# A sort of edges by matrix products: its table of next places kept as three bf16 parts and brought up to date by the vector engine

## The reference

```python
edge_index = jnp.stack([src, dst])
# in the first layer: row, col = edge_index
out = jax.ops.segment_sum(msg, row, num_segments=N)      # grouped by src
```

## Time and profile before

| | us |
|---|---|
| median of 3 runs | 12618.34 (12607.03 to 12618.74) |
| the profiled execution | 12618.56 |
| its span in the profile | 12616.8 |
| mean granted clock of PE, share of full speed | 0.591 |
| busy: POOL / DVE / PE / ACT | 6532.0 / 5345.2 / 3962.2 / 2582.5 |

### The profile page before, as it was taken

One profiled execution on the slowest core, in us unless ns is written; L12 is line 12 of the kernel. 1 busy time (PEld: TensorE's weight loads), 2 busy tenths in 40 slices (PEclk: granted clock), 3 DMA queues, 4 the chain that ended last, 5 costly groups with the idle time before them and its releaser, 6 DMA issues. The chain is left out here.

```text
span 12616.8 us, 82629 instructions
## 1 busy us (share of the span) xinstructions
PE 3962.2 (31%) x19153; PEld 2596.1 (21%) x19153; DVE 5345.2 (42%) x6339; ACT 2582.5 (20%) x3818; POOL 6532.0 (52%) x6784
## 2 busy tenths in 40 slices
PE   2667501896333333344000100010002000015877
PEld 2555401453111111244000100010001000003544
DVE  6222285334555555277455322222223466652111
ACT  0333253232222322111000011100110233320000
POOL 0666576002777777374777477747773655540000
PEclk9555555897555555577555555555555555557899
DMA  6000022666888888200666311121111222225899
GB/s 276 3 3 3 12 91 78 230 269 229 270 265 267 266 265 270 55 0 0 176 188 187 67 38 37 36 20 38 37 37 18 60 80 80 81 70 200 323 384 359
DMA packets 586456, 1693.37 MB, mean 134 GB/s; under 512 B 267163, under 2 KB 321858, under 8 KB 568289
## 3 DMA queue, kind: packets, MB, share of 16 engines
q0 software_dynamic: 292720, 608.23, 18.7%
q1 hardware_dynamic: 229648, 722.30, 15.7%
q10 hardware_dynamic: 63952, 361.30, 7.3%
HBM read 1016.07 MB, written 675.24 MB: 134 GB/s over the span
## 5 line engine op out<-in xcount | busy, mean ns | idle before, releaser
L1991 POOL DMA_INDIRECT ring<-tab_gat,at x2352 | 2235.8, 951 | 1082.5 <-issue 719.7
L706 POOL DMA_INDIRECT ring<-z_stn,at x1568 | 1508.2, 962 | 1406.2 <-POOLq L703 912.0
L2159 PE MATMUL keys<-spot,ones 128*128 128x128 f32 x6 | 2.3, 487 | 3766.2 <-PEq L2158 3766.2
L1503 PE MATMUL pair_acc<-pair_w,pair_cell 32*112 32x384 f32 (+1 forms) x1120 | 780.3, 878 | 1261.3 <-PEq L1500 1261.3
L560 POOL DMA_INDIRECT sorted<-rows,at x784 | 759.3, 968 | 761.8 <-POOLq L558 528.5
L706 POOL DMA_INDIRECT ring<-z_conv,at x784 | 767.4, 979 | 386.7 <-issue 249.9
L1082 POOL DMA_INDIRECT adj<-val_a,at_a x784 | 766.0, 977 | 335.3 <-issue 255.2
L1249 PE MATMUL acc<-tile,parts 128*96 128x448 f16 (+1 forms) x3430 | 729.4, 361 | 257.5 <-DVE parts L1173 139.8
L2159 PEld LDWEIGHTS keys<-spot,ones 128*128 128x128 f32 x6 | 1.5, 311 | 3766.9 <-issue 3766.9
L2085 DVE COPY peak<-peak 128x6 f32<-128x6 f32 x112 | 19.8, 176 | 1672.4 <-DVEq L2084 1672.4
L878 PE MATMUL acc<-tail,hot 128*128 128x49 f32 (+4 forms) x588 | 145.8, 432 | 1797.9 <-PEq L876 1797.9
(11 more groups left out here) (453 smaller groups left out, 10619.7 us busy)
## 6 DMA issues: line engine op xcount, KB each, us to landing
tile<-adj SPq DMA_DIRECT2D x490, 784.0 KB, 21.4
z_stn<-block ACTq DMA_DIRECT2D x245, 800.0 KB, 3.3
z_conv<-pair_block ACTq DMA_DIRECT2D x224, 700.0 KB, 6.2
run_gat<-out_rows SPq DMA_DIRECT2D x56, 1596.0 KB, 5.5
adj<-zero SPq DMA_DIRECT2D x49, 1568.0 KB, 38.6
run_basis<-out_rows SPq DMA_DIRECT2D x28, 1750.0 KB, 5.8
ring<-tab_gat,at POOLq DMA_INDIRECT x2352, 2.4
run_gat<-out_rows SPq DMA_DIRECT2D x56, 672.0 KB, 3.1
```

Of the source, the lines that this page charges most:

```text
L706: g.indirect_dma_start(out=view(bufs[b], k), out_offset=None, in_=table, in_offset=bass.IndirectOffsetOnAxis(ap=at[n][b][:, k:k + 1], axis ...
L1503: last = pe.matmul(self.acc[g][0:self.nodes, n, 0:(hi - lo) * self.fo], self.cell[:, :], cols, start=True, stop=True)
L1991: g.indirect_dma_start(out=ring[b][:, k, :], out_offset=None, in_=tab_gat, in_offset=bass.IndirectOffsetOnAxis(ap=at[b][:, k:k + 1], axis= ...
```

## The change

The table of next places, `first`, stays in SBUF in f32, and beside it stands a copy as three bf16 tiles, `parts`: the rounded value, the rounded rest, and the rest of that. DVE makes them (`split`), and DVE adds the lap's sums to the table too: PE's product with the identity and ACT's copy of the table are gone. The f32 look-up product becomes three bf16 products, one for each part, and ACT copies each transposed unit only once, as bf16. PE waits at the head of a lap for `parts_ready` instead of `table_ready`.

```diff
-                lo_rows = sb(st, "lo_rows", [P, ST, P])
-                lo_rows_b = sb(st, "lo_rows_b", [P, ST, P], BF16)
+                lo_rows = sb(st, "lo_rows", [P, ST, P], BF16)
+                parts = [sb(st, f"parts{b}", [P, 3, ST, NT], BF16) for b in range(2)]
+                rest = sb(st, "rest", [P, ST, NT])
@@ DVE @@
+                    def split(b):
+                        v.tensor_copy(parts[b][:, 0, :, :], first[b][:, :, :]).then_inc(dve_step, 1)
+                        v.wait_ge(dve_step, 1)
+                        v.sem_inc(dve_step, -1)
+                        v.tensor_tensor(rest[:, :, :], first[b][:, :, :], parts[b][:, 0, :, :], ALU.subtract).then_inc(dve_step, 1)
...
+                        v.tensor_copy(parts[b][:, 1, :, :], rest[:, :, :]).then_inc(dve_step, 1)
...
+                        v.tensor_tensor(parts[b][:, 2, :, :], rest[:, :, :], parts[b][:, 1, :, :], ALU.subtract).then_inc(dve_step, 1)
...
+                        v.sem_inc(sem("parts_ready"), 1)
@@
-                    v.sem_inc(sem("first_made"), 1)
-                    v.sem_inc(sem("table_ready"), 1)
+                    split(0)
                     v.sem_inc(sem("found_free"), 1)
                     make(0, 0)
                     with v.Fori(0, steps) as it:
                         for b in range(2):
                             make(1 - b, it * 2 + b + 1)
+                            v.wait_ge(sem("table_summed"), 1)
+                            v.sem_inc(sem("table_summed"), -1)
+                            v.tensor_tensor(halves(first[1 - b]), wide(table), halves(first[b]), ALU.add).then_inc(dve_step, 1)
+                            v.wait_ge(dve_step, 1)
+                            v.sem_inc(dve_step, -1)
+                            split(1 - b)
                             v.wait_ge(sem("found_ready"), 1)
@@ ACT @@
-                            a.wait_ge(sem("table_summed"), 1)
-                            a.sem_inc(sem("table_summed"), -1)
-                            a.copy(halves(first[1 - b]), wide(table)).then_inc(act_step, 1)
...
-                            a.sem_inc(sem("table_ready"), 1)
                             def take(lo, hi):
...
-                                a.copy(lo_rows_b[:, lo:hi, :], turned[:, 0:hi - lo, :])
                                 a.copy(lo_rows[:, lo:hi, :], turned[:, 0:hi - lo, :]).then_inc(act_step, 1)
@@ PE @@
-                    def carried(b):
-                        for h in range(2):
-                            pe.matmul(table[:, h, 0:half * NT], ident[:, :],
-                                      first[b][:, h * half:(h + 1) * half, :].rearrange("p j k -> p (j k)"), start=True, stop=False)
...
                             take("hot_made")
-                            take("table_ready")
-                            carried(b)
-                            summed(b, True).then_inc(sem("table_summed"), 1)
+                            take("parts_ready")
+                            for j in range(ST):
+                                last = pe.matmul(cell(table, j), hot_lo[b][:, j, :], hot_hi[b][:, j, :], start=True, stop=True)
+                            last.then_inc(sem("table_summed"), 1)
...
                             for j in range(ST):
-                                pe.matmul(cell(found, j), lo_rows[:, j, :], first[b][:, j, :], start=True, stop=False)
+                                for k in range(3):
+                                    pe.matmul(cell(found, j), lo_rows[:, j, :], parts[b][:, k, j, :], start=(k == 0), stop=False)
                                 last = pe.matmul(cell(found, j), earlier[:, j, :], hot_hi[b][:, j, :], start=False, stop=True)
```

More of the change, by code:

```diff
@@ L452, in _ @@
                         for b in range(2):
-                            a.wait_ge(sem("table_summed"), 1)
-                            a.sem_inc(sem("table_summed"), -1)
-                            a.copy(halves(first[1 - b]), wide(table)).then_inc(act_step, 1)
-                            a.wait_ge(act_step, 1)
-                            a.sem_inc(act_step, -1)
-                            a.sem_inc(sem("table_ready"), 1)
                             def take(lo, hi):
@@ L483, in _ @@
                 def _(pe):
[L485 to L488, removed]
                     for h in range(2):
@@ L497, in _ @@
                             pe.sem_inc(sem("hot_made"), -1)
-                            summed(b, False).then_inc(sem(f"hot_free{b}"), 1)
+                            for j in range(ST):
+                                last = pe.matmul(cell(table, j), hot_lo[b][:, j, :], hot_hi[b][:, j, :], start=False, stop=False)
+                            last.then_inc(sem(f"hot_free{b}"), 1)
                     for h in range(2):
@@ L506, in _ @@
                     pe.matmul(cell(found, 1), ones[:, :], deg[:, :], start=True, stop=True).then_inc(sem("digits_summed"), 1)
-                    pe.wait_ge(sem("first_made"), 1)
-                    pe.sem_inc(sem("first_made"), -1)
-                    def carried(b):
-                        for h in range(2):
-                            pe.matmul(table[:, h, 0:half * NT], ident[:, :],
-                                      first[b][:, h * half:(h + 1) * half, :].rearrange("p j k -> p (j k)"), start=True, stop=False)
                     def turn(b, lo, hi):
@@ L523, in match @@
                         for j in range(lo, hi):
-                            last = pe.matmul(gram[:, j - lo, :], lo_rows_b[:, j, :], lo_rows_b[:, j, :], start=False, stop=(j == hi - 1))
+                            last = pe.matmul(gram[:, j - lo, :], lo_rows[:, j, :], lo_rows[:, j, :], start=False, stop=(j == hi - 1))
                         last.then_inc(sem("gram_ready"), 1)
```

## The result

| | before | after |
|---|---|---|
| median, us | 12618.54 (12607.03 to 12621.81) | 12415.55 (12393.57 to 12423.62) |
| profiled execution, us | 12618.56 | 12409.41 |
| its span | 12616.8 | 12407.7 |
| first and last scatter of the sort, us | 297.06 and 1523.38 | 290.83 and 1332.97 |
| one lap of 14 scatters | 22.00 | 18.65 |

The ratio is 0.9838, with an interval of 0.9821 to 0.9855: 203 us less. The forecast was 12408.0, within 12386 to 12512.

A forecast was written before the change was run, and what follows sets the result against it. PE and ACT together were taken to set the 22.0 us lap, with POOL next at 17.8. 12618.6 less 218.6 (train of scatters) and 5.3 (start), plus 13.3 (slower scatters), gives 12408.0 us; range 12386 to 12512.

The forecast's parts named there:

- The bound: Sort loop: PE and ACT set the 22.0 us lap; afterwards POOL's 14 scatters, 17.8 us, would; 80 in 100.
- PE and ACT: Their lap in the sort falls to 13.1 us mean: 0.65 + 9.95 + 2.5, the last for 56 bf16 products.
- rival 1: Look-ups: PE stays the bound, products in one cell 0.169 us apart; lap 20.1, about 12512 us; 9 in 100.
- rival 3: Look-ups: each product waits for its predecessor in the cell, 0.244 us; lap 24.3, 12747 us; 4 in 100.
- DVE: Table update adds 4.85 us a lap, at most 5.6; DVE's lap 11.1 us, beside PE, so not the bound.
- The start: Before the loop: splitting the first table costs 3.7 us, yet the first scatter comes at 291.7, 5.3 us earlier.
- The cost on POOL: Scatters beside DVE's new SBUF work: 17 ns longer each, 784 of them, 13.3 us.
- The bound of 76 us: Upper bound of the scatters' slowing: 0.34 us for each of four new DVE operations, 56 x 1.36.
- rival 2: POOL is locked out for the whole of DVE's four new operations: 156 us, total 12551 us; 5 in 100.
- The pauses: Sort's scatters: at each 112th the next comes after 3.18 us, not 1.27; six times 1.91, 11.5 us.
- The sum: Whole kernel: 12618.6 - 218.6 - 5.3 + 13.3 = 12408.0 us; all behind the sort moves as a whole.
- Its own mark for a failure: Sort loop in the profile after: laps over 18.5 us would be wrong; 17.8 to 18.1 us were expected.

The follow-up runs named there:

- psum: Changed kernel with sum, rest and second rest written in place in PSUM, one more copy to SBUF; second run 12371.82 us, ratio 0.9817.
- update_only: Changed kernel without parts: DVE still sums the table, look-ups f32, ACT copies each unit twice; first 13777.69 us, second 12459.38 us, ratio 0.9887.
- e1_after: The changed kernel again, unedited, as measure for two edited kernels beside it; the three took 13795.95, 13800.91 and 13804.26 us.
- lookup_only: Changed kernel with PE's carried product and ACT's table copy kept; look-ups bf16, DVE splits the table; 13825.77 us, ratio 1.0006.
- pe168: Changed kernel with 168 more bf16 look-up products a lap, results overwritten; first 14105.15 us, second 12447.04 us, ratio 0.9871.
- second look at the kernel before: The kernel before the change, run once more unedited for its trace; 12612.74 us.
- rest_psum: Changed kernel with only the rest kept in PSUM, so the second subtraction has one SBUF input; one of 13795.95, 13800.91 and 13804.26 us.
- eight long runs: First series of follow-up runs, where every kernel took 1200 us or more longer; the kernel before took 13806.51 and 13828.79 us.

## Why the prediction was right, and where it was not

**The bound.** Right: PE's and ACT's chain gave way to POOL, DVE's wait moved to the free rank buffer, and the list of a lap is ready long before POOL wants it (written at 814.43 for the lap that begins at 831.69).

**PE and ACT.** Right in each term. PE and ACT from 804.56, with the table load in it:

```profile
804.56 0.74 PE L537 MATMUL table<-hot_hi,hot_lo 128*128 128x49 bf16 x14 [5.84 <-PEq L531]
...
805.84 1.28 ACT L477 ACT_TABLE_LOAD   x1 [10.03 <-ACTq L476]
...
815.93 0.28 PE L551 MATMUL found<-parts,lo_rows 128*128 128x49 bf16 x3 [0.92 <-PEq L531]
...
816.04 0.22 PE L552 MATMUL found<-hot_hi,earlier 128*128 128x49 bf16 x1
...
816.20 0.22 PE L552 MATMUL found<-hot_hi,earlier 128*128 128x49 bf16 x1
...
818.20 0.22 PE L552 MATMUL found<-hot_hi,earlier 128*128 128x49 bf16 x1
```

A group of four products comes every 0.167 us in the mean (816.04 and 816.20 are two of them), so 41 to 42 ns each where 44 were assumed, and the 56 take 2.3 us. That they go to one cell costs nothing, and with that rivals 1 (0.169 us) and 3 (0.244) fall. The lap from the first sum to the end of the look-ups (818.20, and one product more) is 13.7 us; the prediction's 0.65 + 10.6 + 2.5 is 13.75.

**DVE.** Right, a little high: the update takes from 799.97 to 804.27, 4.3 us for 4.85, because 0.15 us lie between the steps, not 0.24. The casts took 549 and 520 ns, as the row of another shape gave it.

**The start.** First scatter at 290.83 for 291.7, 6.2 us earlier than before, for 5.3.

**The cost on POOL.** This is the term that was mis-sized. Said were 17 ns a scatter, 13.3 us; the 777 ordinary gaps have a mean of 1.3209 for 1.2723, 37.8 us. The bound of 76 us held it. The prediction had both rows, the mean of 985 ns and the single scatter of 1.31, and took the mean of the other stage, with the words "a similar number of such operations per time". That premise is the step that failed, in two ways. First, the number: in that stage only one operation of this length with both inputs in SBUF (L2311, last section) comes for 13 scatters, where the change adds two for 14; the long ones there, of 3.8 and 7.4 us, have an input in PSUM and hold none. Second, the meeting: of its 27 operations 13 stopped a scatter, where here 103 of 108 do. DVE is released by the scatters through the rank buffer, so its update begins at nearly the same distance behind a lap's first scatter each time (released at 814.12, scatter at 813.04), and the same two subtractions meet the same two scatters. Counted from the first scatter, the seventh and the eighth of each fourteen are in the mean 1.541 and 1.608 us ahead of the next, the sixth 1.317, and all others 1.27 to 1.28. Two hits a lap at the 0.34 us of the single scatter would have been 56 x 0.68 = 38 us. Had the two subtractions met the scatters by chance, it would by my estimate have been 34 us: 112 of them, each over a scatter's 0.13 us with a chance of 0.875 / 1.272, for half its length in the mean. So that there are two of the kind in a lap weighs more here than that their phase is tied. The experiment with `psum` shows it from the other side: with no such operation the train is 36.6 us shorter and each place of a lap has 1.27. By the Trainium skill, "SBUF — State Buffer", section "SBUF: two separate sides", the ports are locked by whichever begins first, for the whole of its instruction. The trace agrees on the side of the subtraction (the scatter goes on 0.83 to 0.85 us behind its end) and on the condition of two SBUF inputs, but not on the whole length: a scatter is stopped only at certain points, and 62 subtractions that began 0.16 to 0.18 us behind a scatter, in seven of the runs, ran over it in their ordinary 0.87 to 0.88 us without a delay to either. So rival 2, with its whole length of all four operations, falls: 37 us, not 156.

**The pauses.** At each 112th scatter the next comes 2.63 us later and not 3.18, so six of 1.36 for 1.91: 3.3 us less. It was 3.17 to 3.18 in five runs in which POOL waited between laps (both looks at the kernel before, the second of `update_only`, `e1_after`, `lookup_only`), and 2.62 to 2.63 in the three in which it didn't (the changed kernel and the second runs of `psum` and `pe168`); why is open.

**The sum.** Its own mark for a failure, laps over 18.5 us, was passed (18.65), as was 1300 to 1315 for the last scatter (1332.97). The time came out at 12409.4 for 12408.0 because three misses cancel: the train 21.1 us longer than said (1042.1 for 1021.0), the start 0.9 earlier, and all behind the last scatter 18.7 us shorter (11074.7 for 11093.4), which the prediction had moved as a whole. Nothing of the change is there. The same stretch took 11087.0 in the second look at the kernel before, and 11064.0, 11090.0 and 11110.4 in `psum`, `update_only` and `pe168`; what moves it by 20 to 45 us between kernels that don't differ there stays open. So the agreement to 1.4 us is luck: the part that the change touches was said 20 us too short.

## What to carry to other kernels

Where an engine of the chain is relieved, look for the engine whose gaps aren't counted as busy (here POOL, 0.97 us and 0.30 idle per scatter): its own pace is the floor, and 89% of the shorter lap was reached by the change's cheapest part. When a cost comes from two engines meeting, don't take a mean from elsewhere: count the operations of the kind that meets, there and here (an input in PSUM takes one out of the count), and ask whether a semaphore ties their phases, since then the same ones meet in every lap. An operation on DVE with both inputs in SBUF beside scatters of POOL is better given one input in PSUM, if DVE has the time: here it was worth 37 us of train.

## What the runs showed of the hardware

**Holding a scatter.** A scatter of 0.97 us is stopped at about 0.13 us by a DVE operation with two SBUF inputs until this ends: 52 of 52 and 51 of 51 in the changed kernel, and again by L395 in 52 of 52 in `pe168`. A cast from SBUF to SBUF that runs there does it too if it came first by enough. Over seven runs 113 casts from SBUF to SBUF began at most 0.12 us ahead of a scatter: the 73 that began 0.044 us or more ahead stopped it, for 0.27 to 0.35 us; the 40 that began later didn't, and took 0.55 to 0.6 us for 0.52 themselves. A cast that runs in the scatter's last part adds 0.16 (26 of 26 in `rest_psum`); the 62 subtractions over the same last part added nothing. Operations with an input in PSUM held none: in `psum`, where each of the update has one, the first of 784 scatters alone is long, and that one is also in the kernel before (1.20 us).

The stage behind the sort shows the same in the kernel before, with other operations. DVE and POOL around the long scatter of the earlier trace rows:

```profile
1608.93 0.89 DVE L2311 TENSOR_TENSOR hat<-hat 128x700 f32<-128x700 f32 x1
1609.35 1.31 POOL L1082 DMA_INDIRECT adj<-val_a,at_a  x1 [0.30 <-issue]
1609.97 3.80 DVE L2316 TENSOR_TENSOR sums<-hat_bank,hat 128x3500 f32<-128x3500 f32 x1
1610.97 0.97 POOL L1082 DMA_INDIRECT adj<-val_a,at_a  x1 [0.30 <-issue]
```

L2311 has both inputs in SBUF; it ends at 1609.82 and its scatter at 1610.66, 0.84 later, and 13 of the 13 scatters of that window (1560 to 2060 us) that have it over their 0.13 us are long. Of the two inputs of L2316, 3.8 us long, `hat_bank` is a PSUM tile (L2289), and of the scan L818, 7.4 us long, `decay` is (L689): none of the 78 and none of the 159 scatters under them is long.

**The clock.** The column of `update_only` says 1.00 for its stretch, in the windows; below it stands one row of PE in order of time:

```profile
270.00:1358.00 1088.00, 731.22 (x4872) 600.49 (x4928) 335.31 (x449) 374.54 (x700) 761.71 (x784) 1.00 0.03 3
```

```profile
899.78 0.60 PE L504 MATMUL turned<-unit_b,hot_lo 128*128 128x128 bf16 x4
```

and yet four turning products take 0.60 us, as before at 0.56 of full speed (and 823.89 in the earlier trace rows); where `pe168` was at the upper level they take 0.38:

```profile
829.34 0.38 PE L519 MATMUL turned<-unit_b,hot_lo 128*128 128x128 bf16 x4
```

The trace of `update_only` has no record of the clock in that stretch. The durations decide, not the column.

**Waiting for instructions.** In the eight long runs the lap was 24.0 to 24.6 us for six of the kernels, whatever the kernel did in it, and the spacing of scatters still 1.27. PE, DVE and ACT of `e1_after`:

```profile
818.80 0.34 PE L537 MATMUL table<-hot_hi,hot_lo 128*128 128x49 bf16 x4 [0.26 <-issue]
820.24 0.37 PE L537 MATMUL table<-hot_hi,hot_lo 128*128 128x49 bf16 x5 [1.10 <-issue]
821.67 0.34 PE L537 MATMUL table<-hot_hi,hot_lo 128*128 128x49 bf16 x4 [1.06 <-issue]
...
828.95 0.87 DVE L452 TENSOR_TENSOR prod<-found,hot_hi 128x686 f32<-128x686 f32 x1 [12.93 <-DVEq L451]
```

Fourteen products that otherwise go in 0.6 us come in batches of four or five with 1.1 us of "issue" between, and the product of DVE starts 10.6 us after the look-ups it waited for were done (818.4). With 84 and 168 more products a lap the laps grew to 26.79 and 29.58, 26 and 30 ns for each further product against the 24.59 of `e1_after`. That they waited for the instruction stream is my reading of these rows; what brought the condition on, and took it away on the same chip later, is open.
